# Sixty scatters ahead of the edge rows, a first list of six groups, and a first stage that sums gathered rows until six beats past its sweep

## The reference, cut to what matters

```python
agg = segment_sum(x[src], dst)            # two SAGE layers (divided by degree)
agg = segment_sum(norm * x[src], dst)     # three GCN layers
x = segment_sum(w * x[src], dst)          # L3: 3 layers x 3 hops, w = dinv[src]*edge_weight*dinv[dst]
out = out + x @ W[l, k]
y = layernorm(h + out) * gamma + beta; h = relu(y)
```

## Time and profile before

| | |
|---|---|
| median of 3 runs | 6878.76 us (6877.93 to 6886.88) |
| the profiled execution: own time / span | 6887.01 / 6885.1 us |
| busy PE / weight loads / VectorE / ScalarE / GpSimd | 6183.2 / 3701.9 / 2158.9 / 309.1 / 4719.0 us |
| PE idle before line 1051 for `counts`, 700 to 3100 us | 184.3 us, 170.1 of them at once |
| first scatter of the lists / first gather of stage 0 | 222.78 / 1150.44 us |

### The profile page before, as it was taken

The page is one execution under the profiler, slowest core; times in us unless marked ns, Lnnn a source line. Parts: engine busy times, 40 slices in busy tenths (PEclk is TensorE's granted clock), DMA queues, the critical chain, the costliest instruction groups (busy, mean ns, idle before and its releaser), DMA issues.

```text
span 6885.1 us, 79487 instructions
## 1 busy us (share of the span) xinstructions
PE 6183.2 (90%) x27391; PEld 3701.9 (54%) x27592; DVE 2158.9 (31%) x8268; ACT 309.1 (4%) x843; POOL 4719.0 (69%) x4959
## 2 busy tenths in 40 slices
PE   0499752999999999989999999999999999999998
PEld 0399521655555555545655555555555555655555
DVE  8644720223322221212222233222223322222244
ACT  0000000000000000000000000000000000000000
POOL 0677777566666667667677676776767767677676
PEclk9999976999999999999999999999999999999999
DMA  9475332666666767778888888888888888888887
GB/s 359 173 310 224 97 97 77 202 195 203 181 195 184 213 199 217 218 247 288 283 290 290 294 296 288 280 286 279 296 295 289 291 286 280 285 292 291 300 295 231
DMA packets 582180, 1703.64 MB, mean 247 GB/s; under 512 B 163490, under 2 KB 325467, under 8 KB 479392
## 3 DMA queue, kind: packets, MB, share of 16 engines
q1 hardware_dynamic: 316850, 1337.88, 56.9%
q0 software_dynamic: 157584, 240.14, 12.2%
q10 hardware_dynamic: 107388, 120.98, 5.0%
HBM read 1476.43 MB, written 223.40 MB: 247 GB/s over the span
## 4 chain that ended last, share of the span: by engine, by line
PE 61%; POOL 15%; DMA 13%; issue 11%; DVE 0%; POOLq 0%; SPq 0%; ACT 0%; ACTq 0%; DVEq 0%
PE pwide L1055 33%; PE pwide L1051 16%; PE pstep L1084 9%; POOL ring_f L655 7%; POOL counts L629 6%; DMA ring_f<-table,f_src 5%; DMA counts<-lane_val,lane_idx 3%; DMA counts<-zz 3%; POOL weights L629 1%; PE pwide L1142 1%; DMA weights<-lane_val,lane_idx 1%; PE pwide L1141 0%; PE pwide L1100 0%; PE pwide L1137 0%; PE pwide L1065 0%
## 5 line engine op out<-in xcount | busy, mean ns | idle before, releaser
L655 POOL DMA_INDIRECT ring_f<-table,f_src x3492 | 3322.0, 951 | 1518.3 <-issue 916.0
L1055 PE MATMUL pwide<-room,acc 128*128 128x512 f32 (+1 forms) x3920 | 1759.0, 589 | 19.8 <-DMA room<-weights 19.8
L1055 PE MATMUL pwide<-room,hcur 128*128 128x512 f32 (+1 forms) x3136 | 1405.9, 588 | 0.0
L1084 PEld LDWEIGHTS pstep<-hot,ring_f 128*128 128x128 f32 x7272 | 1000.3, 192 | 536.0 <-issue 372.7
L1619 DVE TENSOR_SCALAR hot<-iota,f_win,f_wgt 128x64 f32<-128x64 f32 x2916 | 729.8, 334 | 1550.6 <-PE pstep L1084 1534.2
L1084 PE MATMUL pstep<-hot,ring_f 128*128 128x64 f32 x7272 | 974.1, 267 | 110.9 <-DMA ring_f<-table,f_src 109.5
L1051 PE MATMUL pwide<-room,hcur 128*128 128x512 bf16 (+1 forms) x3154 | 892.1, 367 | 187.2 <-DMA room<-counts 182.6
L1055 PEld LDWEIGHTS pwide<-room,acc 128*128 128x128 f32 x3920 | 704.5, 191 | 654.7 <-issue 604.9
L1051 PE MATMUL pwide<-room 128*128 128x512 bf16 (+1 forms) x2635 | 953.9, 367 | 2.5
L629 POOL DMA_INDIRECT counts<-lane_val,lane_idx x720 | 707.6, 983 | 220.0 <-issue 204.8
L1055 PEld LDWEIGHTS pwide<-room,hcur 128*128 128x128 f32 x3136 | 562.9, 191 | 505.3 <-issue 465.4
(11 more groups left out here) (309 smaller groups left out, 2403.2 us busy)
## 6 DMA issues: line engine op xcount, KB each, us to landing
room<-weights SPq DMA_DIRECT2D x700, 1024.0 KB
room<-counts SPq DMA_DIRECT2D x600, 512.0 KB
room<-weights SPq DMA_DIRECT2D x156, 768.0 KB
weights<-zz SPq DMA_DIRECT2D x56, 1792.0 KB
counts<-zz ACTq DMA_DIRECT2D x44, 1568.0 KB, 8.5
ring_f<-table,f_src POOLq DMA_INDIRECT x3492
room<-weights SPq DMA_DIRECT2D x56, 512.0 KB
table<-acc ACTq DMA_DIRECT2D x56, 256.0 KB
```

What stands on the lines that cost most here:

```text
L655: pool.indirect_dma_start(out=ring_f[:, slot, :], out_offset=None, in_=rows_from[:, :], in_offset=bass.IndirectOffsetOnAxis(ap=f_src[:, c: ...
L1055: ins = pe.matmul(bank[:, 0:w * P], x_of(a)[:, first + o, :], room[:, n % SLOTS, o * w * P:(o + 1) * w * P], start=begins, stop=ends)
L1084: ins = pe.matmul(bank[:, low:low + WIN], row, one, start=begins, stop=ends and not own, skip_group_check=True)
```

## The change

The scatters of list 0 are now also issued ahead of the edge rows: its first 60 go in front of the 21 gathers and of the verdict, after waits for `lanes_ready` 1 and for the zeroes of six groups (24 transfers). `scatter` is moved up so that it can be called there. CUT becomes 6: list 0 holds six groups (556 - 132 = 424 scatters, 8 laps), list 1 the other five (832 - 532 = 300 scatters, 6 laps), 724 scatters in all against 720. `FIRST` gets lead 108 and trail -6: batches at beats 108 to 186, the last three (beats 183, 184 and 186) within stage 1's sweep. `EARLY` gets lead 12, trail 8: batches at beats 12 to 170. The waits added to `whole` are on the way that this graph does not take.

```diff
-FIRST = Split([4, 4], [4] * 10 + [1], 100, 2)
-EARLY = Split([4, 4], [4] * 10 + [1])
+FIRST = Split([4, 4], [4] * 10 + [1], 108, -6)
+EARLY = Split([4, 4], [4] * 10 + [1], 12, 8)
...
-CUT = 5
+CUT = 6
+AHEAD_OF_ROWS = 60
...
-LISTS = [Lanes(132, 484, 8, EARLY.ns * P, (EARLY.ns + 4 * CUT) * P),
-         Lanes(464, CHUNKS, 8, (EARLY.ns + 4 * CUT) * P, N),
+LISTS = [Lanes(132, 556, 8, EARLY.ns * P, (EARLY.ns + 4 * CUT) * P),
+         Lanes(532, CHUNKS, 6, (EARLY.ns + 4 * CUT) * P, N),
...
+            def scatter(which, i):
+                p, m = LISTS[which], (weights if which == 2 else counts).rearrange("s (n a) -> (s n) a", a=1)
...
+            pool.wait_ge(lanes_ready, 1)
+            wait_zeroed(pool, zeroed_counts, ZQ, 4 * CUT)
+            for i in range(AHEAD_OF_ROWS):
+                scatter(0, i)
+
             pool.wait_ge(off_ready, 1)
             pool.wait_ge(e_out, 96)
             blocks = [(k, rows_d.bitcast(I32), e_dst) for k in range(RBLOCKS)]
...
             def fast():
-                for which in range(2):
-                    pool.wait_ge(lanes_ready, which + 1)
-                    wait_zeroed(pool, zeroed_counts, ZQ, EARLY.zeros_short if which else 4 * CUT)
-                    for i in range(LISTS[which].lane):
-                        scatter(which, i)
+                for i in range(AHEAD_OF_ROWS, LISTS[0].lane):
+                    scatter(0, i)
+                pool.wait_ge(lanes_ready, 2)
+                wait_zeroed(pool, zeroed_counts, ZQ, EARLY.zeros_short)
+                for i in range(LISTS[1].lane):
+                    scatter(1, i)
...
             def whole(way):
+                for q in range(LISTS[0].laps):
+                    pool.wait_ge(scattered[q], len(range(q, AHEAD_OF_ROWS, LISTS[0].laps)) * 16)
```

More of the change, by code:

```diff
@@ L607, in _ @@
                 pool.memset(lows[:, :, c:c + 1], float(LOWS[c])).then_inc(g_lows, 1)
[L609 to L618, removed]
             def scatter(which, i):
@@ L631, in scatter @@
                     in_=lane_val[which][:, at:at + 1], in_offset=None).then_inc(scattered[q], 16)
-            def fast():
-                for which in range(2):
-                    pool.wait_ge(lanes_ready, which + 1)
-                    wait_zeroed(pool, zeroed_counts, ZQ, EARLY.zeros_short if which else 4 * CUT)
-                    for i in range(LISTS[which].lane):
-                        scatter(which, i)
+            pool.wait_ge(lanes_ready, 1)
+            wait_zeroed(pool, zeroed_counts, ZQ, 4 * CUT)
+            for i in range(AHEAD_OF_ROWS):
+                scatter(0, i)
+            pool.wait_ge(off_ready, 1)
+            pool.wait_ge(e_out, 96)
+            blocks = [(k, rows_d.bitcast(I32), e_dst) for k in range(RBLOCKS)]
+            blocks += [(k, rows_w, e_wgt) for k in range(RBLOCKS)] + [(k, rows_s.bitcast(I32), e_src) for k in range(WBLOCKS)]
+            for k, rows_, pad in blocks:
+                n = min(RB * CHP, (PAIRS - 1 - k * RB) * CHP + MIX + 3)
+                runs = pad.rearrange("(e a) -> e a", a=1)
+                pool.indirect_dma_start(out=rows_[0:n, k, :], out_offset=None, in_=runs[:, :],
+                                        in_offset=bass.IndirectOffsetOnAxis(ap=off_i[0:n, k:k + 1], axis=0)
+                                        ).then_inc(window_rows if pad is e_dst and k < WBLOCKS else fast_rows, 16)
+            def fast():
+                for i in range(AHEAD_OF_ROWS, LISTS[0].lane):
[4 more added lines that the diff above has]
+                    scatter(1, i)
                 pool.wait_ge(lanes_ready, 3)
```

## The result

The changed kernel takes 6760.6 us (median of four runs, 6757.37 to 6764.63) against 6878.35 us before (four runs, 6870.51 to 6886.88): 117.8 us less, a ratio of 0.9829 [0.9812, 0.9846]. The forecast was 6760. The profiled execution took 6762.21 us with a span of 6760.4, 124.8 us less than that of before. The gain is reached in three steps (the lists end earlier, a group moves into the stall, the waits at the stage borders shrink), and the trace gives each a size.

What follows compares the result with a forecast made beforehand. GpSimd's scatter chain was taken to bound the kernel until 1155 us, PE afterwards. Gains of 57 + 34 + 6 + 22 = 119 us took the profiled 6887.0 to 6768, the median 8.3 lower to 6760; range 6745 to 6797.

Steps and rivals of the forecast that it cites:

- Bound and first step: GpSimd's scatter chain bounds the kernel until 1155 us; the zeroes, not the addresses, set the first scatter, at 132 us.
- Spacing beside two zero transfers: The 60 scatters ahead come 1.286 us apart, take 77 us and end at 209 us.
- crawl: Rival: scatters ahead slow beside two zero transfers or a locked port, ending at 251 us; 6802 us, half of it 6781; chance 0.11.
- a sign of being wrong: The prediction is wrong if, among other signs, the edge rows begin past 220 us; 209 was forecast.
- slower: Rival: scatters ahead wait for slow landings; the gain is gone at 23 us each, 6948 us at 31; chance 0.03.
- Lists: Both lists end earlier: 664 scatters left at 1.288 us, stage 0's gathers begin at 1093 us, 57 us earlier.
- Group 5 into the stall: PE sweeps group 5 while waiting for list 1, so 34 us less remain from its restart to group 9's end.
- Its cover: Group 5 ends at 1034 us, 15 us of delay included, leaving 59 us of cover against list 1.
- GpSimd did not bound stage 0: Rival: the six-lap list or the gathers set stage 0's end, losing 40 or 34 us: 6794 to 6800; chance 0.07.
- Borders: PE's waits for gathered rows shrink: 6 us gained into stage 1, 22 us into stages 2 to 4.
- rows_out: Comes at 1300 us, 91 us earlier than before; some 5 us of stall are left into stage 1.
- Later lead useless: Rival: GpSimd at stages 2 to 4 or list 2's tail takes the 22 us back; 6782 us; chance 0.14.

Runs made afterwards that it cites:

- zeroes_early: Changed kernel with zero transfers begun without the wait for the copied edges and 72 scatters ahead instead of 60: 8752.3 us, 0.9989 against before.
- after_3: The changed kernel, unchanged, run again on chip 8 as the reference for two other runs there: 8743.4 us, 0.9989 against before.

## Why the prediction was right, point by point

- **Bound and first step.** That GpSimd's chain bounded the kernel until 1155 us, and that the zeroes and not the addresses set its new start, held: 135.16 us against 132, ended by `counts<-zz`; `zeroes_early` moved it by moving the zeroes.
- **Spacing beside two zero transfers.** 1.269 us. The rival "crawl" (1.98 us each, edge rows at 251) is refuted in all traces: 1.269 to 1.347. What the experiments did show is a way to late edge rows that the prediction hadn't: not slow scatters, but late offsets from a VectorE that is held. With the same 60 ahead the edge rows began at 230 to 233 us on the other chips, past the 220 that the prediction had set as a sign of being wrong. The rival "slower" needed landings of 23 us and is out.
- **Lists, the term that was too large:** 57 us forecast, 51.0 measured. The start was 3.2 us late, the 60 and the edge rows took 1.7 us less than forecast. The rest is the spacing of the 664 scatters behind the edge rows, 1.2955 us against 1.288, 5.0 us. The mean of 1.288 was made of unlike parts: in PE's stall, with no loads, scatters came 1.262 us apart in both executions, and with that stall 102 us shorter 79 fewer of them do (some 2 us); and beside the loads from 750 to 985 us it was 1.304 against 1.288 (some 3 us). Six laps don't explain the latter: all waits of list 1 for a landing add up to under 1 us more than the usual 0.30 between two. Why it was slower there stays open.
- **Group 5 into the stall:** 34 us in the sum. At group 9's end it was 37.0 against the 34 + 3 forecast there, and the 3 come back behind it. Its cover held: 68.5 us of stall were left. GpSimd did not bound stage 0; its last gather was issued at 1278.67, for a batch that is done near 1296.
- **Borders, the term that was too small:** 28 us forecast, 38.7 measured (35.7 and the 3 us that come back). The waits went as forecast; the clock behind them, an estimate of 8 us, had not been counted.
- **rows_out** came at 1308.6, not 1300. 6.5 of these 8.6 us are the lists'. The first wait was 4.0 us against 5.
- **Later lead useless:** false in the first profile after as far as two traces tell (waits gone, 35.7 us more won by stage 5, the wait for list 2 only 0.6 us longer), true on the chips of the experiments. So that chance of 0.14 depended on where the kernel ran, and nothing in the profile of before told it.

The errors of 6 and 11 us lie on opposite sides, so the total is closer than its terms deserve. It is luck, too, that the median came within a us: for the profiled execution 6768 was forecast and 6762.2 measured, 5.8 less, and the prediction then put the median 8.3 us below that execution, as before, where it lay 1.6 below. What stays open is what holds PE's and VectorE's instructions beside GpSimd's issues in one place and not in the other. Where before takes 6880 us no part of the change was run by itself, so there the sizes of all three steps, and the clock's share, are read from two traces.

## What to carry to other kernels

An engine that is bound by issuing gains what one can move into its idle head, here 51 us of the 59 by which that head shrank, as long as what queues behind it has cover; look for who is late next, since the same scatters made VectorE late on other chips. A stall's price is its wait and the work that is done at the slow clock behind it, here some 2 us for each border. And the gain of a schedule tuned to single microseconds belongs to the place where it was measured: the same change gave 118 us in one place and 12 on two of the other chips, and a part that by its trace helped in the first cost 23 us in the one pair that ran side by side.

## What the runs showed of the hardware

**Instructions held beside indirect DMAs.** On four chips VectorE got about one instruction for each scatter that GpSimd issued, 1.40 us apart, and PE likewise, a weight load and a matmul by turns (126 matmuls beside 286 scatters). In the ten runs with scatters ahead this began for VectorE at 157 to 175 us, 26 to 57 us behind the first scatter. The first two profiles show nothing of it. The page of either kernel lists the instruction transfers, the first profile after like `after_3`:

```profile
q8 instruction: 208, 3.41, 0.2%
```

That is 16.4 KB each. The Trainium skill (Runtime: NRT & Kernel Launch, Instruction fetch mechanics) says that an engine refills its instruction memory in blocks of 16 KiB through a DMA queue of its own, and that this stays hidden because issuing is slower than refilling. The size agrees. Whether it is this path that GpSimd's DMAs hold, no run here shows.

**A whole phase at 1.2 GHz that cost nothing.** In the first profile after, the degree walk ran at half the clock it had before, which the change need not have caused: the granted clock over the whole execution was 0.945 there, and 0.985 in the three other runs of the same kernel, whose times are within 5 us of it. Window of after, then one of before with 50 us:

```profile
400.00:700.00 300.00, 282.38 (x1302) 279.87 (x1303) 136.69 (x682) 0.00 (x0) 228.05 (x234) 0.50 0.67 265
```

```profile
350.00:400.00 50.00, 47.15 (x219) 46.75 (x218) 22.22 (x110) 0.00 (x0) 38.11 (x40) 1.00 0.77 308
```

1302 matmuls in 300 us are 217 in 50, against 219; before did 1303 in the same 300 us. So a granted clock of 0.50 in the page's row of slices isn't by itself a loss; behind the borders, where the sweep's three matmuls took 1.28 us in place of 0.65, it was.
